# Attention pairs closer together in the expert loop, and a sixth expert's weights split ahead of it

## The chip, the cores and the metric

One core of one Trainium2 chip runs the kernel in a single launch. The metric is device time in microseconds (us), the median of several executions. A profiled execution has a span of its own, taken between its first and last instruction; the time of that execution lies a little above its span.

## What is computed

2048 tokens of width 256 (two batches of 1024) pass through one block: a layer norm, then a linear attention and a mixture of experts side by side, both added to the input.

```python
xn = layernorm(x)
# attention, 16 heads of 16
q = k = elu(heads(xn @ Wqk + bqk));  v = heads(silu(xn @ Wv + bv));  u = silu(xn @ Wu + bu)
kv = einsum('bhnd,bhne->bhde', k, v)
attn = (u * layernorm(einsum('bhnd,bhde->bhne', q, kv), g, b)) @ Wo + bo
# experts: 8, the best 2 of each token, hidden width 512
y_e = (silu(xn @ w1_e.T) * (xn @ w3_e.T)) @ w2_e.T
out = x + attn + sum over the two chosen experts of weight * y_e
```

## The kernel before

**Numbers in halves.** Products run in fp16, each fp32 operand being a high half (rounded to fp16) and a low half (the remainder, again fp16); a product takes three matmuls (high-high, high-low, low-high). The weights of an expert are one array of 128 x 3072 fp32. ScalarE (ACT) makes its high half (`hi(e)`, L527), then VectorE (DVE) its low half (`expert_lo(e)`, L748). The halves of expert e land where the fp32 weights of experts e-2 and earlier lay, so `hi(e)` waits for `w_lo` of earlier experts. GpSimd (POOL) later puts gathered rows where the fp32 weights of experts 6 and 7 lay, so its first gather there (tile 8) waits for all eight low halves.

**Front.** Until about 93 us of the span: layer norm, routing, the projections u, k, v, the sums kv, and experts 0 to 4 split. The routing sorts the 4096 (token, expert) entries into tiles of 128 rows of one expert each: 39 tiles (`ST`). The first tiles of experts 1 to 7 are tiles 4, 9, 13, 18, 23, 28 and 32.

**Loop.** Steps t = 0 to 40, written out by hand for each engine; nothing but this order and semaphores decides what runs when. In step t:

- TensorE (PE) does `hidden(t)` (12 matmuls of 512 columns, L1144) and `down(t - 2)` (12 of 256 columns, L1157).
- ACT does `silu(t)` (L608), `h_hi(t)` (L613), and last `y_out(t - 2)` (L625), which scales the result of tile t-2 and puts it into one of `RING` = 8 buffers. `y_out(t)` waits until the add of tile t-8 has landed.
- DVE does `h_mul(t)` (L940) and `h_lo(t)` (L945).
- SyncE (SP) issues the DMA transposes of the hidden rows (`turn_h(t)`) and of the gathered tokens (`load_x(t + 3)`).
- In steps 0, 1 and 2 ACT first does `hi(5)`, `hi(6)`, `hi(7)`, and DVE last does `expert_lo(5)`, `expert_lo(6)`, `expert_lo(7)`.

**Attention in the loop.** The 16 token tiles make 8 pairs. Pair p begins in step `PAIR_AT[p]` (4, 7, 10, ... 25): there PE does `q_kv` (12 matmuls of 128 columns), DVE `center`, `n_rows`, `n_lo`, ACT `n_hi`; one step later ACT does `u_gates`; two steps later PE does `turn`, ACT `y_norm` and `z_hi`, DVE `z_mul` and `z_lo`; three steps later PE does `project` (12 matmuls of 256 columns, L1196) and DVE `finish`.

**GpSimd's queue.** `add_expert(t)` (L461) adds tile t's rows to the output in HBM with an indirect DMA. As adds to the same row must not be in flight together, it waits, beside `y_ready` of its own tile, until all adds of earlier experts have landed (two counts are loaded at L452 for it), and until the add of tile t-2 has landed. In front of the adds of tiles 2 to 9 stand two gathers each (L439: tiles 8 to 23). In front of the adds of the tiles in `FIN_AFTER` (11, 17, 23, 29) stands `add_attention`, a group that waits until every earlier add has landed, issues the adds of two pairs (L470), then up to six gathers (tiles 24 to 29, 30 to 35, 36 to 38, none), and then waits until the two attention adds have landed. A gather of tile t from 24 on also waits until SP's `load_x(t - 16)` has landed. GpSimd's order is thus one chain.

Of the kernel before, what the change touches and what calls it, by code (L numbers as in the profile page):

```python
# [29 lines left out]
ALU = mybir.AluOpType  # L30
ACT = mybir.ActivationFunctionType
# [9 lines left out]
NP = TT // 2  # L41
HD = 16
E = 8
# [20 lines left out]
NEWTON = 3  # L64
RING = 8
GATE_SCALE = 1024.0
EARLY = 5
FEW = 4
PLACES = 16
PAIR_AT = [4 + 3 * p for p in range(NP)]  # L70
FIN_AFTER = {PAIR_AT[2 * i + 1] + 4: (2 * i, 2 * i + 2) for i in range(NP // 2)}
ROUTE_WORDS = 3 * TT * E + 2 * TOPK * TT * E + 6 * TT + TOPK * TT + E * TT + 3 * E + E * E \
    + 2 * ST * (E - 1) + 4 * ST
RSQRT_OPS = 2 + 3 * NEWTON
# [2 lines left out]
def build(nc, x, wattn, wexp, params, bias_rows, out):  # L77
    ctx = ExitStack()
    with ctx:
# [6 lines left out]
        def sem(name):  # L86
            return ctx.enter_context(nc.semaphore(name))
# [126 lines left out]
        attn_lo = sem("attn_lo")  # L214
        w_hi = sem("w_hi")
        w_lo = sem("w_lo")
        shift_ready = sem("shift_ready")
        st_done = sem("st_done")
        mv_done = sem("mv_done")
# [90 lines left out]
        def phase(t, back):  # L310

            return PAIR_AT.index(t - back) if t - back in PAIR_AT else None

# [57 lines left out]
        def _(pool):  # L371
# [60 lines left out]
            def gather(t):  # L432
                if FEW <= t < 2 * FEW:
                    pool.wait_ge(xg_loaded[t % 4], 16)
                if t == 2 * FEW:
                    pool.wait_ge(w_lo, E)
                if t >= 2 * FEW + PLACES:
                    pool.wait_ge(xg_loaded[t % 4], 16 * ((t - PLACES) // 4 + 1))
                g.indirect_dma_start(xgr[place(t)], None, xsplit,  # L439
                                     bass.IndirectOffsetOnAxis(ap=row_in[:, t:t + 1], axis=0)  # L440
                                     ).then_inc(gathered[place(t)], 16)
# [44 lines left out]
        def _(act):  # L486
# [38 lines left out]
            def hi(e):  # L525
                act.wait_ge(raw_loaded[e], 16)
                a.activation(w16[:, e, 0, :], raw(e), ACT.Copy, scale=SCALE).then_inc(w_hi, 1)  # L527

            act.wait_ge(bias_lo, 2)
            hi(0)  # L530
            act.wait_ge(gap_ready, 1)
# [66 lines left out]
            exps(7)  # L598
            halves(6)
            halves(7)  # L600
            a.activation(warm[:], log_scale[:], ACT.Silu).then_inc(warm_done, 1)
            kv_halves(1)

# [11 lines left out]
            def y_out(t):  # L615
                act.wait_ge(y_done, t + 1)
                if t == 0:
                    act.wait_ge(row_gate_ready, 1)
                    for i in range(2):
                        act.wait_ge(kT_done[i], 8 * (TT // CH))  # L620
                if t == 4:
                    act.wait_ge(w_lo, 7)
                if t >= RING:
                    act.wait_ge(y_added[t % 2], 16 * (2 + (t - RING) // 2))
                a.activation(ysb[t % RING], ps_y[t % 2][:, 0:D], ACT.Copy, scale=row_gate[:, t:t + 1]  # L625
                             ).then_inc(y_ready, 1)
# [24 lines left out]
                wait(act, f_done, p)  # L651
                a.activation(z16[:, 0, :], z32, ACT.Copy).then_inc(zh_ready, 1)
            for t in range(ST + 2):
                if t < E - EARLY:
                    act.wait_ge(w_lo, EARLY - 1 + t)
                    hi(EARLY + t)
                if phase(t, 2) is not None:
                    y_norm(phase(t, 2))
                if t < ST:
                    silu(t)  # L660
                if phase(t, 1) is not None:
                    u_gates(phase(t, 1))
                if phase(t, 2) is not None:
                    z_hi(phase(t, 2))
                if t < ST:
                    h_hi(t)
                if phase(t, 0) is not None:
                    n_hi(phase(t, 0))
                if t >= 2:
                    y_out(t - 2)  # L670

        @block.vector
        def _(dve):
# [72 lines left out]
            def expert_lo(e):  # L746
                dve.wait_ge(w_hi, e + 1)
                v.scalar_tensor_tensor(w16[:, e, 1, :], regions[:, (e + 2) * WCOLS:(e + 3) * WCOLS], SCALE,  # L748
                                       w16[:, e, 0, :], ALU.mult, ALU.subtract).then_inc(w_lo, 1)

            def k_map(p):

# [178 lines left out]
            k_lo(7)  # L931
            kv_blocks(1)
            kv_lo(1)


            def h_mul(t):
# [54 lines left out]
            for t in range(ST):  # L991
                if phase(t, 0) is not None:
                    center(phase(t, 0))
                if phase(t, 2) is not None:
                    z_mul(phase(t, 2))
                h_mul(t)
                if phase(t, 0) is not None:
                    n_rows(phase(t, 0))
                h_lo(t)
                if phase(t, 0) is not None:  # L1000
                    n_lo(phase(t, 0))
                if phase(t, 2) is not None:
                    z_lo(phase(t, 2))
                if phase(t, 3) is not None:
                    finish(phase(t, 3))
                if t < E - EARLY:
                    expert_lo(EARLY + t)

        @block.tensor
        def _(pe):  # L1010
# [121 lines left out]

            def hidden(t):

                if t < E:
                    pe.wait_ge(w_lo, t + 1)
                e = expert_of(t)
                pe.wait_ge(xg_loaded[t % 4], 16 * (t // 4 + 1))
                for bank_, col, done, taken in ((ps_a[t % 2], W1, a_done, s_ready), (ps_b[t % 2], W3, b_done, h_ready)):
# [108 lines left out]
```

## Time and profile before

| | us |
|---|---|
| median of 3 runs | 303.94 (302.26 to 304.8) |
| profiled execution | 301.63 |
| its span | 299.9 |
| PE busy | 242.4 (81%) |
| DVE busy | 189.9 (63%) |
| ACT busy | 152.0 (51%) |
| POOL busy | 135.3 (45%) |
| DMA queues, share of 16 engines | q1 (SP's) 52.7%, q0 (GpSimd's) 32.1% |

Busy is the time in which an instruction of the engine runs; it says nothing of what waits for what. A queue entry of GpSimd that issues a DMA counts as busy while GpSimd makes its descriptors; the DMA lands some us later.

### The profile page before, as it was taken

The page shows a single profiled execution, that of the slowest core. Times are in us where ns is not written, and L with a number is a line of the kernel's source. Part 1 is how long each engine was busy: PE and PEld are TensorE (multiplying, and loading weights), DVE is VectorE, ACT ScalarE, POOL GpSimd, SP SyncE. Part 2 cuts the span into 40 slices and gives each one's busy share as a digit, 9 for nine tenths or more (in the row PEclk, how much of TensorE's full clock was granted, in tenths as well). Part 3 has the DMA queues.
Part 4 walks back from the last instruction along what each step waited for, and adds up shares of the span by engine and source line. Part 5 has one row for each costly group of instructions (what it writes and reads, how often), then busy time and mean ns, then how long its engine had stood idle before and what let it go on. Part 6 is the DMA issues. An engine that isn't in the chain of part 4 may idle for free.

```text
span 299.9 us, 6061 instructions
## 1 busy us (share of the span) xinstructions
PE 242.4 (81%) x1784; PEld 158.6 (53%) x1784; DVE 189.9 (63%) x413; ACT 152.0 (51%) x255; POOL 135.3 (45%) x128
## 2 busy tenths in 40 slices
PE   0327998996678886999999999999999979989400
PEld 0117776874455443576666666666566545555200
DVE  3998799499874798685859586867674323333000
ACT  2876784186568661736374545455564323434100
POOL 6375000173300005667874672747265564316561
PEclk9999799999977997999999999999999999999765
DMA  6999992088935339999999999899989999797552
GB/s 209 412 420 407 424 427 107 0 212 237 183 59 76 59 78 119 139 177 146 170 170 130 153 210 127 119 138 178 181 107 152 147 172 124 132 150 109 82 58 32
DMA packets 86290, 50.48 MB, mean 168 GB/s; under 512 B 72547, under 2 KB 83811, under 8 KB 85061
## 3 DMA queue, kind: packets, MB, share of 16 engines
q1 hardware_dynamic: 76516, 35.42, 52.7%
q0 software_dynamic: 9744, 14.69, 32.1%
q8 instruction: 17, 0.28, 0.4%
q14 instruction: 13, 0.10, 0.2%
HBM read 23.35 MB, written 11.67 MB: 117 GB/s over the span
## 4 chain that ended last, share of the span: by engine, by line
PE 29%; DMA 13%; DVE 9%; issue 8%; POOLq 6%; ACT 5%; POOL 1%; ACTq 0%; DVEq 0%
PE bank L1144 16%; PE bank L1157 8%; DMA out<-regions,row_out 5%; POOLq L452 5%; DMA out<-xn 4%; DVE regions L748 3%; ACT regions L527 3%; PE bank L1196 3%; DMA xrow<-xrow 2%; DMA out<-area,row_out 2%; DVE xrow L940 2%; PE bank L1173 1%; PE bank L1185 1%; POOL out L461 1%; DVE xrow L945 1%
## 5 line engine op out<-in xcount | busy, mean ns | idle before, releaser
L1144 PE MATMUL bank<-regions,xg_all 128*128 x468 | 108.9, 384 | 3.9 <-DMA xg_all<-regions 2.1
L1144 PEld LDWEIGHTS bank<-regions,xg_all 128*128 128x128 f16 x468 | 44.6, 99 | 54.7 <-issue 8.2
L1157 PE MATMUL bank<-regions,xrow 128*128 x468 | 59.7, 280 | 7.5 <-DMA xrow<-xrow 7.4
L1157 PEld LDWEIGHTS bank<-regions,xrow 128*128 128x128 f16 x468 | 46.1, 100 | 21.7 <-issue 10.6
L613 ACT ACTIVATE xrow<-xrow 128x512 f16<-128x512 f32 x39 | 24.6, 630 | 58.5 <-DVE xrow L940 58.5
L940 DVE SCALAR_TENSOR_TENSOR xrow<-bank,xrow 128x512 f32<-128x512 f32 x39 | 26.9, 691 | 38.4 <-PE bank L1144 35.2
L461 POOL DMA_INDIRECT out<-area,row_out x20 | 33.6, 1680 | 30.9 <-issue 13.3
L461 POOL DMA_INDIRECT out<-regions,row_out x19 | 31.2, 1643 | 28.7 <-issue 17.5
L439 POOL DMA_INDIRECT xrow<-xsplit,row_in x8 | 11.3, 1408 | 66.4 <-DMA xg_all<-xrow 33.4
L945 DVE TENSOR_TENSOR xrow<-xrow 128x512 f16<-128x512 f32 x39 | 26.9, 690 | 21.6 <-ACT xrow L613 21.6
L608 ACT ACTIVATE xrow<-bank 128x512 f32<-128x512 f32 x39 | 23.2, 595 | 27.7 <-PE bank L1144 27.5
L439 POOL DMA_INDIRECT regions<-xsplit,row_in x31 | 31.0, 1000 | 9.5 <-issue 8.8
L748 DVE SCALAR_TENSOR_TENSOR regions<-regions 128x3072 f16<-128x3072 f32 x8 | 26.8, 3349 | 0.0
L1060 PE MATMUL bank<-wa,xT 128*128 128x256 f16 x192 | 26.4, 293 | 0.0
L527 ACT ACTIVATE regions<-regions 128x3072 f16<-128x3072 f32 x8 | 22.0, 2753 | 2.1 <-DVE regions L748 2.1
L1023 PE MATMUL bank<-ident,xrow 128*128 128x128 f16 x64 | 9.1, 294 | 16.3 <-POOL xrow L420 15.5
L1060 PEld LDWEIGHTS bank<-wa,xT 128*128 128x128 f16 x192 | 18.6, 104 | 7.0 <-issue 4.1
L470 POOL DMA_DIRECT2D out<-xn x8 | 10.2, 1524 | 13.2 <-DMA out<-area,row_out 6.7
L1023 PEld LDWEIGHTS bank<-ident,xrow 128*128 128x128 f16 x64 | 5.3, 125 | 18.0 <-issue 10.4
L1095 PE MATMUL bank<-area 128*128 128x128 f32 x64 | 9.6, 297 | 6.0 <-ACT area L556 6.0
L420 POOL TENSOR_TENSOR xrow<-xn,xrow 128x256 f16<-128x256 f32 x13 | 8.8, 697 | 8.7 <-ACT xrow L497 8.7
L625 ACT ACTIVATE regions<-bank,row_gate 128x256 f32<-128x256 f32 x19 | 8.9, 470 | 6.5 <-PE bank L1157 5.7
(150 smaller groups left out, 304.1 us busy)
## 6 DMA issues: line engine op xcount, KB each, us to landing
regions<-wexp SPq DMA_DIRECT2D x8, 1536.0 KB, 13.9
xsplit<-xrow SPq DMA_DIRECT2D x4, 512.0 KB, 9.6
out<-xn POOLq DMA_DIRECT2D x8, 256.0 KB
area<-x SPq DMA_DIRECT2D x2, 768.0 KB, 7.7
regions<-wattn SPq DMA_DIRECT2D x1, 1032.0 KB, 10.6
xrow<-xrow SPq DMA_TRANSPOSE x39
area<-x SPq DMA_DIRECT2D x1, 512.0 KB, 3.5
regions<-xsplit,row_in POOLq DMA_INDIRECT x31, 4.7
```

The lines of the kernel that those rows point to most:

```text
L439: g.indirect_dma_start(xgr[place(t)], None, xsplit, bass.IndirectOffsetOnAxis(ap=row_in[:, t:t + 1], axis=0)).then_inc(gathered[place(t)], 16)
L452: return pool.value_load(added_before[0:1, i, t:t + 1], min_val=16, max_val=16 * (ST + 1))
L461: g.indirect_dma_start(out, bass.IndirectOffsetOnAxis(ap=row_out[:, t:t + 1], axis=0), ysb[t % RING], None, compute_op=ALU.add).then_inc(y ...
L527: a.activation(w16[:, e, 0, :], raw(e), ACT.Copy, scale=SCALE).then_inc(w_hi, 1)
L608: a.activation(s32[t % 2], ps_a[t % 2][:], ACT.Silu, scale=1.0 / SCALE).then_inc(s_ready, 1)
L613: a.activation(h16[t % 2][:, 0, :], s32[t % 2], ACT.Copy).then_inc(hh_ready, 1)
L748: v.scalar_tensor_tensor(w16[:, e, 1, :], regions[:, (e + 2) * WCOLS:(e + 3) * WCOLS], SCALE, w16[:, e, 0, :], ALU.mult, ALU.subtract).the ...
L940: v.scalar_tensor_tensor(s32[t % 2], ps_b[t % 2][:], 1.0 / SCALE, s32[t % 2], ALU.mult, ALU.mult).then_inc(h_ready, 1)
L945: v.tensor_tensor(h16[t % 2][:, 1, :], s32[t % 2], h16[t % 2][:, 0, :], ALU.subtract).then_inc(hl_ready, 1)
L1060: last = mm(bank_[:, j * D:(j + 1) * D], xT[:, 2 * p + j, KD * d + k, :], wa16[:, w, k * AC + col:k * AC + col + D], start=False, stop=(j ...
L1144: last = mm(bank_[:], xg[t % 4][:, KD * d + k, :], w16[:, bass.ds(e, 1), w, at:at + I].rearrange("p a c -> p (a c)"), start=(k == 0 and n ...
L1157: last = mm(ps_y[t % 2][:, 0:D], hT[t % 2][:, IC * d + c, :], w16[:, bass.ds(e, 1), w, at:at + D].rearrange("p a c -> p (a c)"), start=(c ...
```

## The change

Three things. `PAIR_AT` becomes 4, 7, 9, 12, 14, 17, 19, 22 (alternately 3 and 2 steps apart). `FIN_AFTER` puts the four groups in front of the adds of tiles 9, 14, 19 and 24. Six experts instead of five are split ahead of the loop, and the last two (6 and 7) in halves of 1536 columns, one half in each of steps 0 to 3, on ACT behind `h_hi` and not at the start of the step.

```diff
-EARLY = 5
+EARLY = 6
+HALF = WCOLS // 2
-PAIR_AT = [4 + 3 * p for p in range(NP)]
-FIN_AFTER = {PAIR_AT[2 * i + 1] + 4: (2 * i, 2 * i + 2) for i in range(NP // 2)}
+PAIR_AT = [4 + (5 * p + 1) // 2 for p in range(NP)]
+FIN_AFTER = {PAIR_AT[2 * i + 1] + 2: (2 * i, 2 * i + 2) for i in range(NP // 2)}
...
                 if t == 2 * FEW:
-                    pool.wait_ge(w_lo, E)
+                    pool.wait_ge(late_lo, 2 * (E - EARLY))
...
+            def hi_half(n):
+                e, part = EARLY + n // 2, slice(HALF * (n % 2), HALF * (n % 2 + 1))
+                act.wait_ge(raw_loaded[e], 16)
+                act.wait_ge(w_lo, e - 1)
+                a.activation(w16[:, e, 0, part], raw(e)[:, part], ACT.Copy, scale=SCALE).then_inc(late_hi, 1)
...
             halves(7)
+            act.wait_ge(w_lo, 4)
+            hi(5)
             a.activation(warm[:], log_scale[:], ACT.Silu).then_inc(warm_done, 1)
...
             for t in range(ST + 2):
-                if t < E - EARLY:
-                    act.wait_ge(w_lo, EARLY - 1 + t)
-                    hi(EARLY + t)
...
                     h_hi(t)
+                if t < 2 * (E - EARLY):
+                    hi_half(t)
...
+            def expert_lo_half(n):
+                e, part = EARLY + n // 2, slice(HALF * (n % 2), HALF * (n % 2 + 1))
+                dve.wait_ge(late_hi, n + 1)
+                v.scalar_tensor_tensor(w16[:, e, 1, part], regions[:, (e + 2) * WCOLS:(e + 3) * WCOLS][:, part], SCALE,
+                                       w16[:, e, 0, part], ALU.mult, ALU.subtract).then_inc(late_lo, 1)
...
             kv_lo(1)
+            expert_lo(5)
...
-                if t < E - EARLY:
-                    expert_lo(EARLY + t)
+                if t < 2 * (E - EARLY):
+                    expert_lo_half(t)
```

The other lines follow from these (`y_out` of tile 4 waits for `late_lo` 2, `hidden` of tiles 6 and 7 for `late_lo` 2 and 4).

On DVE, at the entry to the loop, this stood before (L905 is the low half of kv, L940 `h_mul`, L945 `h_lo`, L748 a low half of an expert):

```order
L905 TENSOR_TENSOR kv<-kvm,kv 128x256
L940 SCALAR_TENSOR_TENSOR xrow<-bank,xrow 128x512
L945 TENSOR_TENSOR xrow<-xrow 128x512
L748 SCALAR_TENSOR_TENSOR regions<-regions 128x3072
L940 SCALAR_TENSOR_TENSOR xrow<-bank,xrow 128x512
```

and this stands there now, up to the first attention pair (L921 is the low half of kv, L758 of expert 5, L957 `h_mul`, L962 `h_lo`, L764 a half of a low half, L972 the start of `center`):

```order
L921 TENSOR_TENSOR kv<-kvm,kv 128x256
L758 SCALAR_TENSOR_TENSOR regions<-regions 128x3072
L957 SCALAR_TENSOR_TENSOR xrow<-bank,xrow 128x512
L962 TENSOR_TENSOR xrow<-xrow 128x512
L764 SCALAR_TENSOR_TENSOR regions<-regions 128x1536
...
L957 SCALAR_TENSOR_TENSOR xrow<-bank,xrow 128x512
L962 TENSOR_TENSOR xrow<-xrow 128x512
L764 SCALAR_TENSOR_TENSOR regions<-regions 128x1536
L972 BN_STATS area<-bank 128x6 x2
```

Expert 5's low half moved in front of tile 0's `h_mul`; after each of tiles 0 to 3 a half instruction stands where after tiles 0 to 2 a whole one stood.

On ACT, from the last instruction ahead of the loop's table on, this stood before (L601 is the table load and its warming instruction, L560 the high half of kv, L527 a high half of an expert, L608 `silu`, L613 `h_hi`):

```order
L556 ACTIVATE area<-area 128x512
L601 ACT_TABLE_LOAD
L601 ACTIVATE warm<-log_scale 128x1
L560 ACTIVATE kv<-kvm 128x256
L527 ACTIVATE regions<-regions 128x3072
L608 ACTIVATE xrow<-bank 128x512
L613 ACTIVATE xrow<-xrow 128x512
L527 ACTIVATE regions<-regions 128x3072
```

and this stands there now (L530 is the high half of expert 5, L612 the table, L569 the high half of kv, L619 `silu`, L624 `h_hi`, L536 a half of a high half):

```order
L565 ACTIVATE area<-area 128x512
L530 ACTIVATE regions<-regions 128x3072
L612 ACT_TABLE_LOAD
L612 ACTIVATE warm<-log_scale 128x1
L569 ACTIVATE kv<-kvm 128x256
L619 ACTIVATE xrow<-bank 128x512
L624 ACTIVATE xrow<-xrow 128x512
L536 ACTIVATE regions<-regions 128x1536
```

Expert 5's high half moved ahead of the table load; the halves stand behind `h_hi`, so that the low half of a step can only begin after that step's `h_hi`.

On GpSimd, around the first group, this stood before, from the gathers of tiles 22 and 23 and the add of tile 9 to the add of tile 11 (L439 gather, L452 the two counts, L461 add of a tile, L470 adds of the attention):

```order
L439 DMA regions<-xsplit,row_in 128x512 x2
...
L461 DMA out<-area,row_out 2304x256
...
L461 DMA out<-area,row_out 2304x256
L470 DMA out<-xn 128x2x256 x2
L439 DMA regions<-xsplit,row_in 128x512 x6
L452 TENSOR_LOAD added_before
L452 ISA x2
```

and this stands there now, from the add of tile 8 to that of tile 9 (L464 add of a tile, L473 adds of the attention, L442 gather, L455 the counts):

```order
L464 DMA out<-area,row_out 2304x256
L473 DMA out<-xn 128x2x256 x2
L442 DMA regions<-xsplit,row_in 128x512 x8
L455 TENSOR_LOAD added_before
L455 ISA x2
```

The group moved up by two adds and took the gathers of tiles 22 and 23 behind its own six. The other three groups moved up by three, four and five adds and are otherwise as they were.

## Rows read from the trace of the kernel before

**Rows 1.** The page, busy time of each engine and its share of the span.

```profile
PE 242.4 (81%) x1784; PEld 158.6 (53%) x1784; DVE 189.9 (63%) x413; ACT 152.0 (51%) x255; POOL 135.3 (45%) x128
```

**Rows 2.** Timeline of GpSimd: start, us, line, operation, tiles, idle before and releaser.

```profile
124.20 1.84 POOL L461 DMA_INDIRECT out<-area,row_out  x1 [1.87 <-ACT area L625]
...
152.82 1.91 POOL L461 DMA_INDIRECT out<-area,row_out  x1 [0.30 <-issue]
...
159.60 1.62 POOL L461 DMA_INDIRECT out<-area,row_out  x1 [2.32 <-issue]
161.74 1.57 POOL L461 DMA_INDIRECT out<-area,row_out  x1 [0.52 <-issue]
166.34 2.56 POOL L470 DMA_DIRECT2D out<-xn  x2 [3.02 <-DMA out<-area,row_out]
...
177.57 1.70 POOL L461 DMA_INDIRECT out<-area,row_out  x1 [0.62 <-issue]
179.72 1.56 POOL L461 DMA_INDIRECT out<-regions,row_out  x1 [0.45 <-issue]
186.94 1.56 POOL L461 DMA_INDIRECT out<-regions,row_out  x1 [5.67 <-issue]
...
209.90 1.81 POOL L461 DMA_INDIRECT out<-area,row_out  x1 [0.57 <-ACT regions L625]
217.01 1.58 POOL L461 DMA_INDIRECT out<-area,row_out  x1 [5.30 <-DMA out<-area,row_out]
...
226.23 1.56 POOL L461 DMA_INDIRECT out<-regions,row_out  x1 [0.30 <-issue]
...
240.12 1.63 POOL L461 DMA_INDIRECT out<-regions,row_out  x1 [2.70 <-issue]
```

**Rows 3.** The same timeline, the last adds.

```profile
274.90 1.55 POOL L461 DMA_INDIRECT out<-regions,row_out  x1 [0.47 <-DMA out<-regions,row_out]
279.58 1.54 POOL L461 DMA_INDIRECT out<-area,row_out  x1 [3.13 <-DMA out<-regions,row_out]
...
292.16 1.55 POOL L461 DMA_INDIRECT out<-regions,row_out  x1 [0.72 <-DMA out<-regions,row_out]
```

**Rows 4.** Timeline of all engines, end of the loop: last `down`, two of `y_out`.

```profile
278.21 0.47 ACT L625 ACTIVATE regions<-bank,row_gate 128x256 f32<-128x256 f32 x1 [0.84 <-DMA out<-regions,row_out]
...
280.91 2.74 PE L1157 MATMUL bank<-regions,xrow 128*128 x12 [2.74 <-DMA xrow<-xrow]
...
283.69 0.47 ACT L625 ACTIVATE regions<-bank,row_gate 128x256 f32<-128x256 f32 x1 [5.00 <-PE bank L1157]
```

**Rows 5.** Timeline of all engines, entry to the loop.

```profile
92.31 1.28 ACT L601 ACT_TABLE_LOAD   x1
93.61 0.20 ACT L601 ACTIVATE warm<-log_scale 128x1 f32<-128x1 f32 x1
...
94.68 0.42 ACT L560 ACTIVATE kv<-kvm 128x256 f16<-128x256 f32 x1 [0.87 <-DVE kvm L900]
...
95.13 0.43 DVE L905 TENSOR_TENSOR kv<-kvm,kv 128x256 f16<-128x256 f32 x1 [0.48 <-ACT kv L560]
...
98.33 0.69 DVE L940 SCALAR_TENSOR_TENSOR xrow<-bank,xrow 128x512 f32<-128x512 f32 x1 [2.78 <-ACT xrow L608]
99.06 0.63 ACT L613 ACTIVATE xrow<-xrow 128x512 f16<-128x512 f32 x1 [0.83 <-DVE xrow L940]
99.60 2.75 ACT L527 ACTIVATE regions<-regions 128x3072 f16<-128x3072 f32 x1
```

**Rows 6.** The same timeline, tiles 1 to 4 and the `y_out` of tile 2.

```profile
105.59 3.35 DVE L748 SCALAR_TENSOR_TENSOR regions<-regions 128x3072 f16<-128x3072 f32 x1
...
108.86 0.68 DVE L940 SCALAR_TENSOR_TENSOR xrow<-bank,xrow 128x512 f32<-128x512 f32 x1
...
116.10 0.76 DVE L955 BATCH_NORM_STATS2 area<-bank 128x6 f32<-128x256 f32 x2
...
121.44 0.46 ACT L625 ACTIVATE area<-bank,row_gate 128x256 f32<-128x256 f32 x1
```

More of the change, by code:

```diff
@@ L216, in build @@
         w_lo = sem("w_lo")
+        late_hi = sem("late_hi")
+        late_lo = sem("late_lo")
         shift_ready = sem("shift_ready")
@@ L621, in y_out @@
                 if t == 4:
-                    act.wait_ge(w_lo, 7)
+                    act.wait_ge(late_lo, 2)
                 if t >= RING:
@@ L1133, in hidden @@
             def hidden(t):
-                if t < E:
+                if t < EARLY:
                     pe.wait_ge(w_lo, t + 1)
+                elif t < E:
+                    pe.wait_ge(late_lo, 2 * (t + 1 - EARLY))
                 e = expert_of(t)
```

## The prediction

> **What bounds the kernel now.** I read the page first. TensorE is busy for 81% of the span and GpSimd for 45% [rows 1], and whoever stops there takes TensorE for the bound. The timelines of the end say otherwise. TensorE's last matmuls, the `down` of tile 38, start at 280.91, and ACT hands that tile over at 283.69 + 0.47 = 284.16 [rows 4]. GpSimd issues the add of the same tile only at 292.16 [rows 3]. At the front GpSimd needed 2.30 us from a handed-over tile (121.44 + 0.46 = 121.90) to its add (124.20) [rows 2, 6]; by that the last add could have gone out at 286.5, so GpSimd is 5.7 us behind. Behind the last add lie another 299.9 - 292.16 = 7.7 us until it has landed and the kernel ends.
>
> Next I followed GpSimd's timeline back to where it last waited for work. The add of tile 2 at 124.20 is held by ACT (1.87 us idle, released by L625). After it I find short waits, or waits for adds to land: 2.32 in front of tile 9, 3.02 in front of the first attention adds, 5.67 in front of tile 13, 5.30 in front of tile 18 [rows 2]. These are the first tiles of new experts, and the groups, where every earlier add must have landed. A second sign is in ACT's row at 278.21: the `y_out` of tile 37 is held by the landing of an add 8 tiles back [rows 4], so the ring of result buffers is full at the end. From tile 2 on, then, the kernel is GpSimd's chain of adds, gathers and landings. TensorE feeds it and is ahead. A change reaches the time by (a) moving the add of tile 2, where the chain hangs on ACT, or (b) changing the chain's own length from there.
>
> **The change at the entry to the loop (a).** Before, `h_mul` of tile 0 starts at 98.33 [rows 5]. Now expert 5's high half (2.75) stands ahead of the table load: the load moves from 92.31 to 95.06, and with 1.28 + 0.20 + 0.42 for the load, the warming instruction and the high half of kv, DVE's low half of kv can start near 96.97 in place of 95.13 [rows 5]. It takes 0.43. Expert 5's low half follows, 3.27 from its start to the next instruction's (105.59 to 108.86 [rows 6]). `h_mul` of tile 0 then starts at 96.97 + 0.43 + 3.27 = 100.7, 2.3 later. Its `silu` (no longer behind a conversion) is done by then and hides there.
>
> Then four rounds, one for each of tiles 0 to 3. Each is now `h_mul` to `h_hi` 0.73 (98.33 to 99.06), `h_hi` to the next ACT instruction 0.54 (99.06 to 99.60) [rows 5], half a high half, half a low half, and the next `h_mul`. No row has 1536 columns, so both halves lie between rows: ACT between 0.63 at 512 columns and 2.75 at 3072, on a line 1.47; DVE between 0.69 and 3.35 [rows 5, 6], on a line 1.75, of which 0.08 overlaps the next instruction as in the whole one. A round is 0.73 + 0.54 + 1.47 + 1.67 and twice 0.03 between engines = 4.47. As the half waits for `h_hi`, ACT and DVE work one after the other; before, the conversion on ACT ran a step ahead. Four rounds put the first `center` at 100.7 + 17.9 = 118.6, where it started at 116.10 [rows 6]: **2.5 us later**. I take the line, since 1536 lies between the two lengths; if a half took just half of the whole (1.38 and 1.68), a round would be 0.16 shorter and the shift 1.9. I put it at +2.4, bounds +1.5 to +3.2.
>
> The page "VectorE: DVE Perf Modes" of the Trainium skill (section on the TRN2 errata) speaks against halving: it says an instruction on SBUF data pays a fixed latency once, however long it is, and that fp32 two-operand operations take (N + 151)/0.96 ns. By it a half would be an estimated 1.757 us, four of them 0.31 us more than two whole ones; the line through the rows gives 0.3, so the trace agrees and the sum stays.
>
> What hangs on that `center`: `h_mul` of tile 4, `y_out` of tile 2 behind them on ACT, and so the add of tile 2, which goes from 124.20 to 126.6. The gather of tile 8 needs the last half at 118.6, and the adds of tiles 0 and 1 stand ahead of it anyway, so it is no second term. Nothing later gives the 2.4 us back, because GpSimd is never again ahead of its data.
>
> **The chain from tile 2 on (b).** The number of adds, gathers, attention adds and counts loaded is the same. What differs is which waits coincide. Before, the group in front of tile 23 coincided with an expert's first tile, and paid once. Now the group in front of tile 9 does, and tile 23 pays by itself.
>
> - First group. Before: tile 8 to 9 took 159.60 - 152.82 = 6.78 (two gathers inside and only 2.32 idle, the wait being hidden behind them), tile 10 to 11 with the group took 177.57 - 161.74 = 15.83 [rows 2]. Now: tile 8 to 9 takes 15.83 plus the two gathers without a wait to fill, 6.78 - 2.32 - 2.15 = 2.31, and tile 10 to 11 a plain 2.15 (177.57 to 179.72). Difference 18.14 + 2.15 - 6.78 - 15.83 = -2.3.
> - Second group: tiles 13 to 14 instead of 16 to 17, same six gathers; they trade places with a plain step, 0.
> - Third group: before, tile 22 to 23 took 240.12 - 226.23 = 13.89 and 18 to 19 a plain step [rows 2]. Now 18 to 19 takes the 13.89, and 22 to 23 a lone wait. Lone waits took 186.94 - 179.72 = 7.22, 217.01 - 209.90 = 7.11 [rows 2] and, when TensorE and the transposes had ended, 279.58 - 274.90 = 4.68 [rows 3]. Tile 23 lies in the busy part: 6.8, between them but near the first two. Against a plain 2.2 that is +4.6 (bounds +2.5 and +5.0).
> - Fourth group, in front of 24 instead of 29: it trades places with a plain step, 0.
>
> Sum **+2.3**, bounds 0 (if the lone wait costs as in the quiet end and landings vary my way) to +4. That the last group comes five tiles earlier gives nothing by itself: GpSimd has the same list still to do and is behind throughout.
>
> **Pairs closer together.** In steps 9, 14 and 19 one pair begins and the previous one is turned, so DVE gets 0.69 + 0.69 more there, and `project` of the next step may stand about 1 us. Three such stops are 3 us on TensorE. Cover: the 5.7 us by which the last add trails its data, which grows by (b), to 8.0. Without this cover they would come onto the path. Also the ring: with the fourth group in front of tile 24 its add goes out near 259, and `y_out` of tile 32 must wait for its landing, some 2 us; this too falls on ACT and TensorE.
>
> **Sum.** 299.9 + 2.4 + 2.3 = 304.6 span, 306.3 for such an execution (301.63 before). The median of the runs lies 2.3 above the profiled execution; with the same 2.3 it is 308.6, and I say **308.5**, 1.5% slower. (About 1% is what a measurement of this kernel tells from no change.)
>
> **The rivals.**
>
> 1. *Only one term comes* (the halves overlap better than my rounds, or the lone wait at tile 23 costs little, as the 4.68 in rows 3 would have it). Span 299.9 + 2.3 to 2.4, time 306.3: no change by the 1%.
> 2. *Faster: GpSimd catches up.* For it: plain steps are not constant, they wait for the landing of the add two tiles back (row at 292.16: 0.72 released by a DMA [rows 3]); after the last group 14 adds follow instead of 9. If landings in that stretch get short enough, GpSimd meets TensorE before tile 38, and the end is ACT's last hand-over: 284.16 + 2.4 + 2.3 + 7.7 = 296.6 span, median 300.6, or 298.2 if the front costs nothing. It decides when the chain gets 3.3 us shorter from tile 2 on, where I have it 2.3 longer. Against it: GpSimd's own 1.55 and the counts in each step don't shrink. The page "DMA: Bandwidth & Descriptors" (section on latency and other measured facts) says that a landing in HBM costs less under light load; rows 3 with 4.68 against 7.22 agree. By that rule the waits moved ahead into the busy part would cost more, and the freed end less; the number of lone waits does not fall.
> 3. *TensorE becomes last*, by the full ring and the doubled steps: ACT's last hand-over would have to come after 292.16 + 4.7 - 2.3 = 294.6, 10.4 us later than now, of which 2.4 + 3 + 2 are accounted for. If it lost 6 more, span 307.5, median 311.5.
>
> **How the numbers follow.** Forecast 0.57, rival 1 0.23, rival 2 0.13, rival 3 0.07. The forecast's own range is 306 to 311.5; a tenth of the whole falls within 1% of it (below 307). Faster by over 1%: rival 2, less the part that stays within 1%, 0.12. Within 1%: rival 1, 0.10 of the forecast and 0.01 of rival 2, less 0.04 of rival 1 beyond it: 0.30. Slower: 0.58. For 8 in 10 the range leaves out rival 2 and the far end of rival 3: 302.5 to 312.
>
> **What would show it.** Right: the first `center` near 118.6; the add of tile 2 near 126.6; a lone wait of 6 to 7 us in front of tile 23; the last add 10 us or more behind ACT's last hand-over; `y_out` of tile 32 held by a DMA. Wrong: rounds shorter than 4.3; GpSimd's plain steps below 2.0 between tiles 24 and 38; the last add released by ACT's L625, which would be rival 2 or 3.

## The result and the profile after

| | before | changed |
|---|---|---|
| median (runs) | 304.37 us (4) | 309.32 us (4) |
| lowest to highest | 302.26 to 305.17 | 307.84 to 312.15 |
| ratio, 95% interval | | 1.0248 (1.018 to 1.0316) |
| profiled execution, its span | 301.63, 299.9 | 312.15, 310.4 |

The change makes the kernel slower. The ratios, here and in the table of the experiments, leave out disturbed executions and the medians don't, and the profiled execution of the changed kernel is the slowest of its four, so its span overstates the difference. A second profile of it, among the experiments (e13), has a span of 304.7. I use both.

Busy times, from the page of the profile (engine, us, share of the span, instructions):

```profile
PE 250.0 (81%) x1784; PEld 160.5 (52%) x1784; DVE 190.0 (61%) x415; ACT 152.3 (49%) x257; POOL 135.7 (44%) x128
```

DVE, ACT and POOL are within 0.4 us of before, although the time is not. TensorE's 250.0 is 7.6 us more than before in this profile, but 243.1 in e13, 0.7 more; the mean granted clock was 0.939 here, 0.954 in e13 and 0.950 before. So the busy times don't tell where the time went.

Timeline of all engines of the changed kernel, entry to the loop (start, us, line, operation, tiles, idle before and releaser; L565 is the last conversion of k, the last instruction of ACT that the change left alone):

```profile
93.26 0.61 ACT L565 ACTIVATE area<-area 128x512 f32<-128x512 f32 x1
93.78 2.75 ACT L530 ACTIVATE regions<-regions 128x3072 f16<-128x3072 f32 x1
...
96.54 1.28 ACT L612 ACT_TABLE_LOAD   x1
...
101.99 0.68 DVE L957 SCALAR_TENSOR_TENSOR xrow<-bank,xrow 128x512 f32<-128x512 f32 x1
102.71 0.63 ACT L624 ACTIVATE xrow<-xrow 128x512 f16<-128x512 f32 x1 [3.51 <-DVE xrow L957]
103.24 1.47 ACT L536 ACTIVATE regions<-regions 128x1536 f16<-128x1536 f32 x1
...
104.75 1.76 DVE L764 SCALAR_TENSOR_TENSOR regions<-regions 128x1536 f16<-128x1536 f32 x1 [0.68 <-ACT regions L536]
...
106.42 0.68 DVE L957 SCALAR_TENSOR_TENSOR xrow<-bank,xrow 128x512 f32<-128x512 f32 x1
...
119.71 0.75 DVE L972 BATCH_NORM_STATS2 area<-bank 128x6 f32<-128x256 f32 x2
```

and the same last conversion of k before:

```profile
91.68 0.61 ACT L556 ACTIVATE area<-area 128x512 f32<-128x512 f32 x1
```

The two executions were already 93.26 - 91.68 = 1.58 us apart where nothing had been changed yet. So the entry has to be measured from that instruction: to the first `center` it took 116.10 - 91.68 = 24.42 us ([rows 6] and above) and now takes 119.71 - 93.26 = 26.45, **2.03 us more**. A round of a tile is 106.42 - 101.99 = 4.43.

Timeline of GpSimd, changed kernel (L464 add of a tile, L473 two attention adds; the first row is tile 2, the second tile 8, then the first group, tiles 9 to 14):

```profile
127.70 2.00 POOL L464 DMA_INDIRECT out<-area,row_out  x1 [2.69 <-issue]
...
157.71 1.62 POOL L464 DMA_INDIRECT out<-area,row_out  x1 [0.30 <-issue]
163.38 2.58 POOL L473 DMA_DIRECT2D out<-xn  x2 [4.05 <-DMA out<-area,row_out]
...
176.62 1.62 POOL L464 DMA_INDIRECT out<-area,row_out  x1 [0.30 <-issue]
178.55 1.57 POOL L464 DMA_INDIRECT out<-area,row_out  x1 [0.30 <-issue]
182.63 1.73 POOL L464 DMA_INDIRECT out<-area,row_out  x1 [2.50 <-DMA out<-area,row_out]
184.80 1.56 POOL L464 DMA_INDIRECT out<-regions,row_out  x1 [0.43 <-issue]
190.44 1.56 POOL L464 DMA_INDIRECT out<-regions,row_out  x1 [4.08 <-issue]
...
206.25 1.64 POOL L464 DMA_INDIRECT out<-regions,row_out  x1 [1.14 <-issue]
...
242.16 1.56 POOL L464 DMA_INDIRECT out<-regions,row_out  x1 [0.45 <-DMA out<-regions,row_out]
247.64 1.56 POOL L464 DMA_INDIRECT out<-regions,row_out  x1 [3.92 <-issue]
...
302.79 1.56 POOL L464 DMA_INDIRECT out<-regions,row_out  x1 [0.52 <-DMA out<-regions,row_out]
```

Tile 2 is added 127.70 - 124.20 = 3.50 us later than in [rows 2], 1.58 of it older than the change, so 1.92 are the change's. From the add of tile 8 to that of tile 38 the chain takes 302.79 - 157.71 = 145.08 us; before it took 292.16 - 152.82 = 139.34 [rows 2, 3]. The lone wait at tile 23 is there (247.64 - 242.16 = 5.48). New beside it are long plain steps such as 182.63 - 178.55 = 4.08, held by the landing of the add two tiles back.

The ends of the two engines, changed kernel, timeline of ACT (hand-over of tile 38) and TensorE (a long stop, in front of tile 27):

```profile
297.42 0.47 ACT L636 ACTIVATE regions<-bank,row_gate 128x256 f32<-128x256 f32 x1 [5.81 <-PE bank L1176]
```

```profile
238.16 4.45 PE L1163 MATMUL bank<-regions,xg_all 128*128 x12 [3.39 <-DMA xg_all<-regions]
```

In this profile TensorE's end moved more than GpSimd's: the hand-over is 297.42 - 283.69 = 13.7 us later [rows 4], the last add 10.6 us. In e13 the hand-over starts at 287.75, only 4.1 us later, and the last add goes out at 297.12. The last add still trails its data, by 302.79 - 297.89 = 4.9 us (8.0 before).

### The profile page after: what moved, and what is told of

It is laid out like the page before. It is cut to its first block and busy times, and to the rows that moved or that the text cites. A ratio compares the mean times of both kernels' runs of the same rounds, so it can differ in the third digit from the quotient of the medians.

```text
span 310.4 us, 6066 instructions
## 1 busy us (share of the span) xinstructions
PE 250.0 (81%) x1784; PEld 160.5 (52%) x1784; DVE 190.0 (61%) x415; ACT 152.3 (49%) x257; POOL 135.7 (44%) x128
## 5 line engine op out<-in xcount | busy, mean ns | idle before, releaser
L1163 PE MATMUL bank<-regions,xg_all 128*128 x468 | 111.5, 390 | 8.6 <-DMA xg_all<-regions 4.5
L1176 PE MATMUL bank<-regions,xrow 128*128 x468 | 58.8, 276 | 7.7 <-DMA xrow<-xrow 7.0
L957 DVE SCALAR_TENSOR_TENSOR xrow<-bank,xrow 128x512 f32<-128x512 f32 x39 | 26.9, 690 | 43.3 <-PE bank L1163 42.9
L624 ACT ACTIVATE xrow<-xrow 128x512 f16<-128x512 f32 x39 | 24.6, 630 | 55.8 <-DVE xrow L957 55.8
L464 POOL DMA_INDIRECT out<-area,row_out x20 | 32.9, 1646 | 41.9 <-issue 26.0
L442 POOL DMA_INDIRECT xrow<-xsplit,row_in x8 | 13.0, 1626 | 67.9 <-DMA xg_all<-xrow 33.5
L464 POOL DMA_INDIRECT out<-regions,row_out x19 | 30.1, 1586 | 26.7 <-issue 14.9
L962 DVE TENSOR_TENSOR xrow<-xrow 128x512 f16<-128x512 f32 x39 | 27.0, 692 | 21.6 <-ACT xrow L624 21.6
L619 ACT ACTIVATE xrow<-bank 128x512 f32<-128x512 f32 x39 | 23.2, 595 | 31.5 <-PE bank L1163 31.2
L442 POOL DMA_INDIRECT regions<-xsplit,row_in x31 | 31.4, 1011 | 9.5 <-issue 9.1
L1077 PE MATMUL bank<-wa,xT 128*128 128x256 f16 x192 | 28.4, 307 | 0.0
L1077 PEld LDWEIGHTS bank<-wa,xT 128*128 128x128 f16 x192 | 19.6, 109 | 8.4 <-issue 4.5
L758 DVE SCALAR_TENSOR_TENSOR regions<-regions 128x3072 f16<-128x3072 f32 x6 | 20.1, 3352 | 0.0
L530 ACT ACTIVATE regions<-regions 128x3072 f16<-128x3072 f32 x6 | 16.5, 2754 | 2.1 <-DVE regions L758 2.1
L473 POOL DMA_DIRECT2D out<-xn x8 | 10.2, 1541 | 12.4 <-DMA out<-area,row_out 6.6
L1040 PEld LDWEIGHTS bank<-ident,xrow 128*128 128x128 f16 x64 | 5.5, 128 | 18.4 <-issue 10.4
```

The lines of the kernel that those rows point to most:

```text
L442: g.indirect_dma_start(xgr[place(t)], None, xsplit, bass.IndirectOffsetOnAxis(ap=row_in[:, t:t + 1], axis=0)).then_inc(gathered[place(t)], 16)
L464: g.indirect_dma_start(out, bass.IndirectOffsetOnAxis(ap=row_out[:, t:t + 1], axis=0), ysb[t % RING], None, compute_op=ALU.add).then_inc(y ...
L619: a.activation(s32[t % 2], ps_a[t % 2][:], ACT.Silu, scale=1.0 / SCALE).then_inc(s_ready, 1)
L624: a.activation(h16[t % 2][:, 0, :], s32[t % 2], ACT.Copy).then_inc(hh_ready, 1)
L957: v.scalar_tensor_tensor(s32[t % 2], ps_b[t % 2][:], 1.0 / SCALE, s32[t % 2], ALU.mult, ALU.mult).then_inc(h_ready, 1)
L962: v.tensor_tensor(h16[t % 2][:, 1, :], s32[t % 2], h16[t % 2][:, 0, :], ALU.subtract).then_inc(hl_ready, 1)
```

## The experiments

All figures of a chain or of the entry are differences of two rows of that kernel's own timeline, in one execution: *entry* from the last conversion of k to the first `center`, *chain* from the add of tile 8 to that of tile 38. The ratio is against the kernel before, run on the same chip.

| kernel | median us | ratio (95%) | entry | chain |
|---|---|---|---|---|
| before | 304.37 | 1 | 24.42 | 139.34 |
| changed | 309.32 | 1.0248 (1.018 to 1.0316) | 26.45 | 145.08 |
| e13 changed, again | 309.51 | 1.0206 (1.013 to 1.0283) | 26.44 | 140.31 |
| e1 weights only | 306.14 | 1.01 (1.0042 to 1.0158) | 26.44 | 139.40 |
| e2 pairs and groups only | 306.98 | 1.0107 (1.0061 to 1.0153) | 23.82 | 144.81 |
| e6 groups only | 310.04 | 1.0178 (1.0116 to 1.024) | 24.72 | 143.76 |
| e7 pairs only | 304.39 | 0.9895 (0.9822 to 0.9968) | 24.72 | 140.41 |
| e3 more TensorE | 305.01 | 1.0059 (1.0015 to 1.0103) | 24.47 | 140.65 |
| e4 groups at 13, 18, 23, 28 | 300.01 | 0.9917 (0.9883 to 0.9952) | 24.31 | 134.92 |
| e5 changed, groups at 9, 13, 18, 23 | 303.38 | 0.9976 (0.9933 to 1.0019) | 26.45 | 137.98 |
| e9 half of the hidden transposes | 300.07 | not given | 23.82 | 132.83 |
| e10 six ahead, whole | 305.02 | 0.994 (0.9855 to 1.0026) | 23.54 | 139.94 |
| e11 e4 with close pairs | 303.91 | 1.0042 (1.0006 to 1.0077) | 24.73 | 139.33 |
| e12 e10 and e11 | 303.77 | 1.0048 (1.0005 to 1.0091) | 23.52 | 140.80 |

The kernel before had medians of 303.35, 303.68 and 303.1 in the three sets (e1 to e4; e5, e6, e7, e9; e10 to e13). A median and its ratio can point different ways (e7, e10). Each entry and each chain is from one execution, so no verdict rests on one of them alone. What executions do by themselves shows in kernels with the same order: the entry of those that leave it alone is 23.82 to 24.73, and the chain of before, e1, e3, e7 and e10, whose groups stand alike, is 139.34 to 140.65.

The stretch from the add of tile 2 to that of tile 8 is in neither column. It took 28.62 before, 30.01 and 31.53 in the two profiles of the change, and 32.00, 30.06 and 31.51 in e3, e4 and e9, which leave the tiles up to there alone. So the 1.4 to 2.9 us by which it is longer in the changed kernel can't be told from chance.

### Which part costs: e1 and e2

e1 is the changed kernel with the pairs and groups of before, e2 the kernel before with those of the change:

```diff
# e1
-PAIR_AT = [4 + (5 * p + 1) // 2 for p in range(NP)]
-FIN_AFTER = {PAIR_AT[2 * i + 1] + 2: (2 * i, 2 * i + 2) for i in range(NP // 2)}
+PAIR_AT = [4 + 3 * p for p in range(NP)]
+FIN_AFTER = {PAIR_AT[2 * i + 1] + 4: (2 * i, 2 * i + 2) for i in range(NP // 2)}
```

> Only the splitting of the weights is changed (six experts ahead of the loop, two in halves); pairs and groups stand as before. Theory (GpSimd's chain is the bound, and it starts late): the first center and the add of tile 2 come 2.0 to 2.4 us later against the last instruction ahead of the loop, and the time is 0.7% (2 us) above before. Rival (the front is hidden by slack, the whole loss is the groups'): the add of tile 2 is late but the time is within 0.3% of before.

> Only the pairs' spacing and the places of the four groups are changed; the weights are split as before. Theory (one more lone wait for landings on GpSimd, at tile 23, and longer plain steps): the time is 3 to 5 us (1.0 to 1.6%) above before, add of tile 2 unchanged, the stretch from add 8 to add 38 about 143 to 145 us against 139.3. Rival (all of the loss is the late start, the groups cost nothing): within 0.5% of before.

e1 costs 1.0%, its entry is 2.0 us longer, its add of tile 2 comes 1.8 us later against the same instruction, and its chain is as before (139.40). e2 costs 1.07%, its entry is not longer. Both rivals fall: each part costs, and 1.0% + 1.07% is what the changed kernel loses in e13 (2.06%), a little less than in its own runs (2.48%).

### Which engine is the bound: e3

```diff
+                    if 9 <= t < 29 and col == W1:
+                        for r in range(1):
+                            mm(bank_[:], xg[t % 4][:, 0, :],
+                               w16[:, bass.ds(e, 1), 0, col:col + I].rearrange("p a c -> p (a c)"),
+                               start=True, stop=True)
```

> The kernel before with one more matmul of 512 columns (its result is overwritten) in the hidden product of tiles 9 to 28: 20 x 0.216 = 4.3 us more of TensorE. Theory (GpSimd's chain is the bound, TensorE is 5.7 us ahead at the end): the time rises by at most 1 us (0.3%), and the gap between ACT's last hand-over and the last add shrinks from 8 us to about 4. Rival (TensorE is the bound, as its 81% suggests): 4.3 us (1.4%) more, gap unchanged.

The extra work reached ACT's last hand-over in full: against the last conversion of k it comes 4.3 us later than before. The time rose by 0.59% (0.15 to 1.03%), 1.8 us, more than the 0.3% that I gave, and the chain's 1.3 us more lie within the spread given above. That is nearer to GpSimd as the bound than to TensorE (1.4%, which the interval leaves out), but it is not nothing. My gap of 4 us did not appear: it was 8.5. In that execution the stretch from add 2 to add 8 was 32.0 us where it was 28.6 before, although the hand-overs of those tiles came at most 0.2 us later, so the last add was late for a reason of its own. The verdict is that the two are coupled: GpSimd's chain ends last, and TensorE's work still reaches it in part.

### Where the groups stand: e6 and e7

e6 moves only `FIN_AFTER` (9, 14, 19, 24), e7 only `PAIR_AT`:

```diff
# e6
+FIN_AFTER = {n: (2 * i, 2 * i + 2) for i, n in enumerate((9, 14, 19, 24))}
# e7
+PAIR_AT = [4 + (5 * p + 1) // 2 for p in range(NP)]
+FIN_AFTER = {n: (2 * i, 2 * i + 2) for i, n in enumerate((11, 17, 23, 29))}
```

> The kernel before with only the four groups moved, in front of tiles 9, 14, 19 and 24; the pairs stay 3 steps apart and the weights are split as before. Theory (the groups' places cost, through GpSimd's waits): all of the 1.07% that pairs and groups cost together is here, 0.8 to 1.4% above before. Rival (the closer pairs cost, through VectorE's doubled steps and the longer stretch without attention): within 0.4% of before.

> The kernel before with only the pairs' spacing changed (alternately 3 and 2 steps), groups in front of tiles 11, 17, 23 and 29. Theory (groups' places cost): within 0.4% of before. Rival (closer pairs cost: steps 26 to 40 have no attention, a step is 3.9 us there in place of 4.7, so the same two transposes come more often and the adds land later): 0.6 to 1.2% above before.

The groups alone cost 1.78%, more than the 0.8 to 1.4% I gave; the close pairs alone cost nothing (ratio 0.9895, but median 0.2% above: no loss, and whether a small gain is left open). So the rival that blames the close pairs falls, and the loss in the loop is the groups' places. e2, which has both, costs less (1.07%) than e6; the two intervals meet, so whether close pairs give part of it back is open.

Two rivals can be settled from these profiles. The groups of e6 did not wait for the attention's own results: the last of the two pairs was finished 11.9 us or more before each group's adds went out. And in e7 ACT hands tile 38 over 6.4 us later than before, against the last conversion of k, with no loss of time: like e3, it says that TensorE is not what sets the time with the groups where they were. Its last add goes out 3.45 us behind the hand-over, so little of that cover was left.

### Do coinciding waits pay once: e4 and e5

```diff
# e4, from the kernel before
+FIN_AFTER = {n: (2 * i, 2 * i + 2) for i, n in enumerate((13, 18, 23, 28))}
# e5, from the changed kernel
+FIN_AFTER = {n: (2 * i, 2 * i + 2) for i, n in enumerate((9, 13, 18, 23))}
```

> The kernel before with the four groups in front of tiles 13, 18, 23 and 28, all of them first tiles of an expert. Theory (a group in front of an expert's first tile pays one wait for landings for two, a lone wait costs 3.4 to 4.6 us over a plain step): three lone waits fewer, at 13, 18 and 28, so GpSimd's chain is 10 to 14 us shorter; the end is then set by TensorE's last tile, which leaves 6 to 8 us: about 296 to 298 us, 2 to 2.7% faster. Rival (the places of the groups don't matter, landings cost what the DMA load makes them cost): within 0.7% of before.

> The changed kernel with its groups in front of tiles 9, 13, 18 and 23, all first tiles of an expert. Theory of coinciding waits: three lone waits fewer than in the changed kernel (at 13, 18, 23), each 3.4 us over a plain step, of which the plain steps give half back as they did with the groups at 13, 18, 23 and 28: 5 us faster than the changed kernel, at 1.2% above to equal with before. Rival (waiting is set by the DMA load alone and only moves): as the changed kernel, 2 to 2.5% above before.

e4 gains 0.83%, e5 brings the changed kernel from +2.1 or 2.5% to -0.24%, even with before. The sign is as the theory has it and the sizes are not. e5 is 2.3 to 2.7% faster than the changed kernel, 7 to 8 us where I had 5. e4's chain is 4.4 us shorter, where three lone waits fewer should have given 10 to 14. GpSimd's timeline of e4, adds of tiles 9 to 12 and the group in front of tile 13:

```profile
160.52 1.62 POOL L461 DMA_INDIRECT out<-area,row_out  x1 [1.79 <-issue]
162.44 1.57 POOL L461 DMA_INDIRECT out<-area,row_out  x1 [0.30 <-issue]
165.90 1.56 POOL L461 DMA_INDIRECT out<-area,row_out  x1 [1.89 <-issue]
168.80 1.56 POOL L461 DMA_INDIRECT out<-regions,row_out  x1 [1.33 <-issue]
174.30 2.55 POOL L470 DMA_DIRECT2D out<-xn  x2 [3.94 <-DMA out<-regions,row_out]
```

Tiles 11 and 12 come 3.46 and 2.90 after the one ahead, not 2.15, because GpSimd had caught up with ACT there: the add of tile 12 goes out 2.5 us after its hand-over began, against 13.0 us before. Work taken away ahead of a point where GpSimd is not behind gives nothing. The rest went into plain steps, whose mean is 2.67 us over e4's 24 of them, 2.25 over the 21 of before (chain less groups and lone waits).

In e5 the last add goes out 2.32 us after its hand-over has ended, no later than at the front (2.30), where ACT held it. So GpSimd had caught up there: at its end e5 is set by TensorE and ACT as well, and more taken from GpSimd's chain could give nothing.

### Does a landing depend on the DMA load: e9

From tile 9 on only the high half of the hidden rows is transposed; the low half of `down`'s input is left over from earlier tiles and not computed.

```diff
+                if t < 9:
...
+                else:
+                    sp.dma_start_transpose(hT[t % 2][:, 0:IC, :], h16[t % 2][:, 0, :]
+                                           ).then_inc(hT_done[t % 2], 16)
```

> The kernel before, but from tile 9 on SyncE transposes only the high half of the hidden rows; the down product uses old low halves in their place, so that part is not computed. The DMA engines have a quarter to a third less to do in the loop; nothing on GpSimd, TensorE, ACT or DVE changes. Theory (how long an add takes to land depends on the load of the DMA engines, and GpSimd's chain on that): plain steps near 2.0 and lone waits near 5 us, chain from add 8 to add 38 6 to 10 us shorter, 2 to 3% faster until TensorE's end sets the time. Rival (a landing takes what it takes, and the waits only depend on the order): chain within 2 us of 139.3 and the time within 0.7%.

The chain is 6.5 us shorter, at the low end of the 6 to 10 that I expected and well outside the 139.34 to 140.65 of the kernels with the same groups, with nothing changed on GpSimd. The median is 1.2% below that of before, where I had 2 to 3%; there is no interval for it. The parts of the DMA view from 200 to 240 us (queue: packets, MB, share of 16 engines), first e9, then before:

```profile
q1 hardware_dynamic: 8627, 2.08, 31.1%
```

```profile
q1 hardware_dynamic: 12696, 3.13, 49.1%
```

With SyncE's share down from 49.1% to 31.1% the lone wait at tile 13 is 5.81 (7.22 before) and the groups sum to 58.0 (60.2). The plain steps did not shrink to the 2.0 that I expected: their mean is 2.24 (2.25 before). The single waits prove little, as the one at tile 13 is 5.86 in e10 with all transposes in place; it is the chain as a whole that says that the waits of GpSimd are partly waits for a loaded DMA system.

### Why the entry is late: e10

```diff
-EARLY = 5
+EARLY = 6
...
             halves(7)
+            act.wait_ge(w_lo, 4)
+            hi(5)
...
             kv_lo(1)
+            expert_lo(5)
```

> The kernel before with six experts split ahead of the loop, but the last two split whole, in steps 0 and 1 at the step's start, as before (pairs and groups as before). Theory (the late entry comes from the halves, whose ACT and VectorE parts run one after the other in four rounds of 4.43 us, and not from expert 5 ahead of the loop): the first center comes about 22.7 us after the last conversion to halves of k (24.4 before, 26.4 changed), the add of tile 2 1.6 us earlier than before, the time 0.3 to 0.7% below before. Rival (expert 5 ahead of tile 0 is what costs): center at 26 us or more after it and the time 0.7 to 1% above before.

Timeline of all engines of e10, the last conversion of k and the first `center`:

```profile
94.92 0.62 ACT L556 ACTIVATE area<-area 128x512 f32<-128x512 f32 x1
...
118.46 0.76 DVE L958 BATCH_NORM_STATS2 area<-bank 128x6 f32<-128x256 f32 x2
```

23.54 us, 2.9 less than with halves; e12 has 23.52. It is 0.9 less than the 24.42 of before but only 0.3 less than the 23.82 of e2 and e9, so a gain over before is not resolved. Expert 5 ahead of the loop does not cost; the halves behind `h_hi` do. e10 undoes both at once, the halving and the place behind `h_hi`, so which of the two costs was not separated. My 22.7 was too low by 0.8, and the add of tile 2 came 0.6 us earlier than before where I had 1.6. The time (0.994, interval across 1) doesn't resolve a gain.

### Both at once, and the changed kernel again: e11, e12, e13

e13 has no edit. e11 is the kernel before with

```diff
+PAIR_AT = [4 + (5 * p + 1) // 2 for p in range(NP)]
+FIN_AFTER = {n: (2 * i, 2 * i + 2) for i, n in enumerate((13, 18, 23, 28))}
```

and e12 is e11 with the edit of e10.

> The kernel before with the pairs alternately 3 and 2 steps apart and the groups in front of tiles 13, 18, 23 and 28; weights as before. Theory (groups' places count, spacing does not): as the kernel with those groups and the old spacing, 0.6 to 1.1% below before, chain from add 8 to add 38 about 135 us. Rival (the closer pairs help by themselves, as the 0.9895 of the spacing alone may say): 1.5 to 2% below before.

> Both together: six experts ahead with the last two whole, close pairs, groups in front of tiles 13, 18, 23 and 28. Theory (start and length of GpSimd's chain add up): 1.1 to 1.8% below before, faster than the kernel before and the changed one. Rival (TensorE's end sets the time once the chain is short): no better than the kernel without the six experts.

> The changed kernel once more, beside the kernel before, on one chip. Theory: 2.0 to 2.5% above before (weights 1.0% and groups 1.1% apart); first center 26.4 us after the last conversion of k; the second plain step behind the groups at 9, 14 and 19 at 3.5 us or more, the lone waits at 13 and 18 near 5.7 us, below the 7.1 of before. Rival (those long plain steps were chance of one execution): plain steps near 2.25 throughout, and the chain from add 8 to add 38 near 142 us.

e11 and e12 fail: they are 0.4 and 0.5% slower than before, so I had not understood how spacing and groups go together. GpSimd's timeline of e11, adds of tiles 9 to 12:

```profile
158.07 1.62 POOL L461 DMA_INDIRECT out<-area,row_out  x1 [1.51 <-issue]
163.26 1.57 POOL L461 DMA_INDIRECT out<-area,row_out  x1 [3.57 <-issue]
167.35 1.56 POOL L461 DMA_INDIRECT out<-area,row_out  x1 [2.52 <-issue]
173.66 1.56 POOL L461 DMA_INDIRECT out<-regions,row_out  x1 [4.75 <-issue]
```

Steps of 5.19, 4.09 and 6.31: here GpSimd waits for tiles. With the first group moved back to tile 13, nothing fills the time in which TensorE is the slower one, and the closer pairs make TensorE slower just there. From add 8 to add 12 e11 takes 21.4 us, e4 14.6, e12 20.8. The hand-overs of tiles 8 to 12 (start to start on ACT) took 22.1 us in e11 and 17.2 in e4; e7, e2 and e12, also with close pairs, have 21.0 to 21.6, and e6 and before, without, 17.1 and 17.4. That explains e11 against e4 in these profiles; it was not tried by itself. No kernel with all its work has a lower median than e4 (300.01); e7's ratio is lower, with an interval that meets e4's.

e13 confirms the entry (26.44) and the sum (2.06%), but on long plain steps it divides. GpSimd's timeline, tiles 8 to 12 of e13:

```profile
156.81 1.62 POOL L464 DMA_INDIRECT out<-area,row_out  x1 [0.30 <-issue]
...
175.17 1.63 POOL L464 DMA_INDIRECT out<-area,row_out  x1 [0.31 <-issue]
177.10 1.57 POOL L464 DMA_INDIRECT out<-area,row_out  x1 [0.30 <-issue]
180.38 1.56 POOL L464 DMA_INDIRECT out<-area,row_out  x1 [1.71 <-DMA out<-area,row_out]
182.45 1.56 POOL L464 DMA_INDIRECT out<-regions,row_out  x1 [0.51 <-issue]
```

The second step behind a group was 4.08, 3.64, 4.51 in the first profile (tiles 11, 16, 21) and 3.28, 2.36, 4.12 here. The lone waits at 13 and 18 were 7.09 and 5.98, against 5.64 and 5.79, and 7.2 and 7.1 before. I had expected all three steps at 3.5 or more. It holds for tile 21 alone in both, and the chain of 140.31 is nearer to the rival's 142 than to 145.08; part of the 145.08 was one execution's chance.

## Why the prediction was right, and where its steps were off

The sign came out as forecast, and so did the two causes. The times, 308.5 against 309.32, agree more closely than the effect does: I had 1.5% slower, and the ratio is 2.48% (1.8 to 3.16), 2.06% (1.3 to 2.83) in e13. The effect was sized too small, and that the two medians lie so close is in part luck of four executions. Step by step:

- **GpSimd's chain is the bound.** Held: in both profiles of the changed kernel the last add goes out 4.9 and 8.9 us after ACT's last hand-over, of e3's 4.3 us of extra TensorE work 1.8 were left in the time (0.5 to 3.1), and of e7's 6.4 none. "Is ahead" was too strong: e3 still cost 0.6%, and in the first profile of the changed kernel TensorE's end moved 13.7 us, beyond the 10.4 that I gave rival 3 as its threshold (4.1 in e13). It did not become last because GpSimd's own end moved 10.6.
- **The entry, +2.4.** Measured +2.0, alike in all four profiles with halves (26.44 or 26.45; changed twice, e1, e5). A round was 4.43 where I had 4.47, the half conversions 1.47 and 1.76 where the line through two rows gave 1.47 and 1.75. The first `h_mul` was 8.73 us behind the last conversion of k and 6.65 before, 2.1 where I had 2.3. The page "VectorE: DVE Perf Modes" of the Trainium skill (section on the TRN2 errata) gives the formula that the prediction cites for the fp32 `tensor_tensor` add alone. The half is a `scalar_tensor_tensor` with fp16 output; its 1.76 measured agrees with the 1.757 estimated by that formula.
- **The chain, +2.3.** The term counts from the add of tile 2. From there to the add of tile 38 the profiles have +7.1 and +3.9, 5.5 in the mean; of that the stretch up to tile 8, which can't be told from chance, has 1.4 and 2.9, and the chain from tile 8 on 5.7 and 1.0, 3.4 in the mean. So the term was too small, by 1 to 3 us, and inside it terms do not match. The first group gave less than the 2.3 foreseen: tile 8 to 9 took 18.91 and 18.36 (18.14 foreseen), and 10 to 11 took 4.08 and 3.28, where the sum had a plain 2.15, which makes +0.4 and -1.0 against before. The lone wait at 23 was 5.48 and 6.14, not 6.8.
- **The plain step.** What failed inside the chain's term is "it trades places with a plain step, 0": a plain step is not one price. It holds the wait for an add two tiles back, and that add lands late behind a group. In the kernel before, the adds next behind the first two groups met a lone wait (tiles 13 and 18: 7.22, 7.11 [rows 2]), which paid for the late landing anyway; that the groups at 9, 14 and 19 leave it to plain steps fits both profiles of the change, but was not taken apart by a run. The timelines of all 14 profiles bear it out as far as they can: the second add behind a group with gathers, where neither it nor the one ahead is an expert's first, took 3.81 us in the mean (2.36 to 5.87, 30 steps; 3.60 at tile 25 before), behind the last group, which has no gathers, 2.51 (14 steps), and in the same place behind a lone wait 2.40 (34 steps). So the late landing goes with the gathers issued in front of the add; no run moved them.
- **Closer pairs are invisible.** Held (e7), with groups where they were. They are not in e11, where GpSimd has caught up. I had them cost TensorE 3 us; in e7 ACT's hand-over of tile 38 is 6.4 later.
- **The doubled steps, 1 us each.** From the starts of `hidden` in the changed kernel's TensorE timeline, less the work inside, steps 9 and 10, 14 and 15, 19 and 20 lose 1.4, 2.6 and 1.4 us, 5.4 where I had 3. It is hidden, as foreseen.
- **The full ring at tile 32.** Did not occur: the add of tile 24 went out at 262.44, but TensorE was late by then too, and the `y_out` of tile 32 came only at 273.00. It did occur in e6, with the same groups and TensorE not slowed by closer pairs, and cost ACT more than the 2 us foreseen. Timeline of ACT of e6, `y_out` of tile 32:

```profile
270.47 0.47 ACT L625 ACTIVATE area<-bank,row_gate 128x256 f32<-128x256 f32 x1 [8.27 <-DMA out<-area,row_out]
```

- **Rival 2's condition.** A slip: it says that GpSimd meets TensorE when the chain gets 3.3 us shorter, but leaves out that the chain itself starts 2.4 later. By the prediction's own terms it is 292.16 + 2.4 - (284.16 + 2.4 + 2.3) = 5.7. The chain got longer, so neither figure was reached.
- **The signs.** Of those named for "right", the first `center` and the add of tile 2 held (2.0 and 1.9 us later against the last conversion of k), the lone wait at 23 held in one profile (6.14) and was short in the other (5.48), and two failed: the last add 10 us or more behind the last hand-over (4.9 and 8.9), and `y_out` of tile 32 held by a DMA.

## What to carry to other kernels

Look for the engine whose queue trails its data at the end, whatever its busy share, and follow it back to where it last waited for work: here most of what moved the time lay before that point, in the queue itself, or in the load on the transfers that it waits for; work of the engine that feeds it reached the time only in part (e3) or not at all (e7). In such a queue waits that everything must drain for should coincide (e4, e5), as long as the queue stays behind its data: where it had caught up (e11, e12) the same move gave nothing. An instruction split in halves to spread its load can cost more than it spreads if each half must follow its partner on another engine within the same step (2.9 us between e10 and the changed kernel, halving and place together).

## What I had not expected of the hardware

- One kernel's executions differ by some us before the loop: the last conversion of k starts at 90.85 and 93.26 in the two profiles of the changed kernel, and at 91.68 before. Two profiles have to be lined up at an instruction that the change left alone, or 1.6 us of chance count as effect.
- The chain of the same kernel took 145.08 us in one profile and 140.31 in another. A difference of a few us between two single profiles of this kernel is not an effect.
- SyncE's transposes lengthen GpSimd's chain: 18 points less of their share of the DMA engines (49.1 to 31.1%) went with 6.5 us less in a chain that holds none of them, where five kernels with all transposes and the same groups lie within 1.3 us of each other.
